# Third layer's feed-forward by rows sorted by position in place of masks, half of its value products on VectorE, and new orders of work

## What is computed

```python
x = L0_attn_representations                     # (2, 1024, 128)
xn = _layernorm(x, axis=-1)
s = _L0_attn_ref(xn, ...)                       # softmax attention, 16 heads, 1024 keys
g = _silu(_L0_ffn_ref(xn, ...))                 # top 2 of 8 experts
x = x + s * g
... L1: linear recurrence, top 2 of 8 experts (hidden 352)
# L2 attention: per token, its 16 heads (of width 8) attend to each other
qkv = jnp.einsum('bnm,fm->bnf', x, Wqkv).reshape(b, n, 16, -1)
scores = jnp.einsum('bnhd,bngd->bnhg', q, k) / SCALE
out = jnp.einsum('bnhg,bngd->bnhd', jax.nn.softmax(scores, axis=-1), v)
return jnp.einsum('bni,mi->bnm', out.reshape(b, n, -1), Wproj) + bproj
# L2 feed-forward: one of 8 matrices, chosen by the token's position alone
idx = jnp.argmax(jnp.einsum('sp,tp->st', pe, jnp.sign(tile_sigs)), axis=-1)
y_all = jnp.einsum('bsd,tod->bsto', x, W) + b
out = take_along_axis(y_all, idx, ...)
... L3: causal attention with decay, top 1 of 8 experts (hidden 512)
```

## Time and profile before

| | |
|---|---|
| median of 3 runs | 991.14 us (988.55 to 994.42) |
| the profiled execution | 985.0 us, its span 983.2 us, granted TensorE clock 0.984 |
| busy: PE, DVE, ACT, POOL | 894.0, 766.7, 537.4, 599.2 us |
| share of the span: PE, DVE, ACT, POOL | 91%, 78%, 55%, 61% |

### The profile page before, as it was taken

How to read it: one execution, slowest core, us unless ns; L and a number is a source line. 1 busy time by engine, 2 the same in 40 slices (tenths; PEclk the granted TensorE clock), 3 DMA queues, 4 the chain that set the end, 5 groups by cost and what they waited for, 6 DMA issues and landing times. The chain is left out here.

```text
span 983.2 us, 20738 instructions
## 1 busy us (share of the span) xinstructions
PE 894.0 (91%) x7627; PEld 471.3 (48%) x7627; DVE 766.7 (78%) x1324; ACT 537.4 (55%) x903; POOL 599.2 (61%) x533
## 2 busy tenths in 40 slices
PE   4899997999999999899998999789999778799996
PEld 2356562233333333233332233679887444478695
DVE  6997789888888888998888852894589999983413
ACT  2154455666766676566666676454365334375463
POOL 3670327668887776878698876106527787572323
PEclk9899998999999999999999999999999999999999
DMA  9362364011111201102111113548761001253562
GB/s 314 117 208 86 105 195 145 16 41 47 32 57 29 65 25 31 49 22 74 40 40 38 40 35 110 169 140 262 217 188 62 23 24 52 68 164 106 161 180 83
DMA packets 90339, 94.86 MB, mean 96 GB/s; under 512 B 23136, under 2 KB 67296, under 8 KB 89984
## 3 DMA queue, kind: packets, MB, share of 16 engines
q1 hardware_dynamic: 85120, 83.04, 27.5%
q0 software_dynamic: 5120, 10.50, 3.7%
HBM read 68.79 MB, written 24.25 MB: 95 GB/s over the span
## 5 line engine op out<-in xcount | busy, mean ns | idle before, releaser
L254 PE MATMUL ps<-ar 64*64 64x512 f32 (+3 forms) x5244 | 518.7, 446 | 28.1 <-DVE small L276 8.9
L254 PEld LDWEIGHTS ps<-ar 64*64 64x64 f32 (+2 forms) x5244 | 254.3, 135 | 275.7 <-ACT ar L300 84.1
L300 ACT ACTIVATE ar<-ps 128x1024 f32<-128x1024 f32 (+1 forms) x302 | 284.0, 944 | 117.5 <-PE ps L254 111.3
L276 DVE TENSOR_REDUCE small<-ps 128x2 f32<-128x1024 f32 (+2 forms) x276 | 306.6, 1139 | 46.6 <-PE ps L254 44.7
L263 POOL TENSOR_TENSOR psum_sb<-psum_sb,ar 128x1024 f32<-128x1024 f32 x91 | 214.8, 2360 | 53.1 <-DVE on_sb L263 41.9
L263 POOL TENSOR_TENSOR ar<-ar 128x512 f32<-128x512 f32 (+1 forms) x80 | 80.0, 1004 | 45.4 <-DVE ar L276 22.3
L322 POOL DMA_INDIRECT gT<-ysort,rt x48 | 48.0, 999 | 92.8 <-issue 91.5
L263 DVE TENSOR_TENSOR ar<-ps,ar 128x256 f32<-128x256 f32 (+4 forms) x48 | 50.5, 1059 | 55.2 <-PE ps L254 51.4
L263 POOL TENSOR_TENSOR psum_sb<-ar 128x1024 f32<-128x1024 f32 x32 | 75.8, 2370 | 23.8 <-ACT ar L300 16.6
L297 ACT COPY ar<-ps 128x256 f32<-128x256 f32 (+2 forms) x84 | 30.8, 378 | 72.7 <-PE ps L254 33.3
L254 PE MATMUL ps<-wA,xnT 128*128 128x512 f32 (+3 forms) x208 | 60.8, 419 | 4.0 <-DVE rt L268 1.8
(11 more groups left out here) (160 smaller groups left out, 1077.2 us busy)
## 6 DMA issues: line engine op xcount, KB each, us to landing
ar<-in_L_up SPq DMA_DIRECT2D x46, 384.0 KB, 4.0
ar<-in_L_b SPq DMA_DIRECT2D x30, 322.0 KB, 3.6
rec_sb<-lscr SPq DMA_DIRECT2D x64, 128.0 KB, 2.9
scr<-ar SPq DMA_DIRECT2D x48, 128.0 KB, 2.6
ar<-xsort SPq DMA_DIRECT2D x36, 128.0 KB, 3.9
ysort<-ar SPq DMA_DIRECT2D x36, 128.0 KB, 1.9
ar<-scr SPq DMA_DIRECT2D x32, 112.0 KB
ar<-scr SPq DMA_DIRECT2D x32, 96.0 KB
```

The source lines that it names most:

```text
L254: return self.e.matmul(o, l, r, start=start, stop=stop) if self.e else Nothing()
L276: return self.e.tensor_reduce(o, a, AX.X, op, negate=True) if negate else self.e.tensor_reduce(o, a, AX.X, op)
L300: return self.e.activation(o, a, fn, **kw) if self.e else Nothing()
```

## The change

The masks of L2's feed-forward go, with `ffn2`, `split` and `combine`. The position's choice is instead routed like an expert (group `BYPOS`), with slots that both halves share; GpSimd scatters the normalised rows (`scat2`), SyncE loads them (`load2`), TensorE turns and multiplies them with one matrix and its bias (`turn2`, `prod2`), ScalarE copies (`xout2`, `yout2`), SyncE stores (`store2`), GpSimd gathers (`gath2`), ScalarE applies Silu (`silu2`). `end2` is now a bias on ScalarE and the blend that the other layers use. VectorE makes the value products of heads 8 to 15 (a new fourth word of `tile`), GpSimd those of 0 to 7. `lnbuf` of L2 has two buffers. All three tables of words are new.

```diff
+BYPOS = NG
+GROUPS += ((2, 0),)
...
+        if layer == 2:
+            return rec_sb[:, 0:512] if c % 2 == 0 else spare[:, 512:1024]
...
-        def ffn2(c):
...
-                    pe.mm(ps[:, b, :], cb_late[:, 128 * e8:128 + 128 * e8], gTT2[:, x_]).then_inc(
...
-                    pe.mm(ps[:, 5, :], w2l[:, 128 * p:128 * p + 128],
-                          psum_sb[:, 512 * (p % 2):512 * (p % 2) + 512], start=p == 0, stop=False).then_inc(
...
+        def turn2(h):
+            for j in range(NTG[BYPOS]):
+                n = NTG[BYPOS] * h + j
+                b = take(ring[0])
+                pe.wait_ge(*vacant(b))
+                pe.wait_ge(*at(f"x2_in{n % 2}", n))
+                for k in range(halves2(j)):
+                    r = slice(128 * k, 128 * k + 128)
+                    ins = pe.tr(ps[:, b, r], xin2[n % 2][:, r], ident)
+                ins.then_inc(*filled(b, ("xT2", n)))
+                yield
...
+        def prod2(h):
...
+                for k in range(halves2(j)):
+                    r, e8 = slice(128 * k, 128 * k + 128), number2[h, j][k]
+                    pe.mm(ps[:, b, r], xT2[n % 2][:, r], w2l[:, bass.ds(e8, 128)], stop=False)
+                    ins = pe.mm(ps[:, b, r], cb_late[0:96, bass.ds(e8, 128)], bias2b[0:96, :], start=False)
...
+            pe.wait_ge(*at(f"tile{k}_dve", i, "av"))
             pe.wait_ge(*at(f"tile{k}_pool", i, "av"))
...
-            dve.stt(acc_sb[:, 1024:1536], ps[:, bank["proj2", c], :], M("bp"), gT[:, cols(c)], ALU.add,
-                    ALU.mult).then_inc(*emptied(("proj2", c), ("gated", 2, c)))
-            yield
-            combine(2, c)
+            blend(2, c)
...
-                dve.tt(xb, x_, ps[:, bank["spread", c, e8], :], ALU.mult).then_inc(
-                    *emptied(("spread", c, e8), ("xb", c, e8)))
...
+            dve.wait_ge(*at(t, i, "shares"))
+            if i >= 2:
+                dve.wait_ge(*at("tileT", i - 2))
...
+            for h in range(8, 16, 4):
+                ins = dve.tt(pr2[k].rearrange("p (g h d) -> p h g d", g=16, d=8)[:, h:h + 4, :, :],
+                             s3_.unsqueeze(3)[:, h:h + 4, :, :].to_broadcast([128, 4, 16, 8]),
+                             qkv[k][:, 256:384].rearrange("p (g d) -> p g d", d=8).unsqueeze(1).to_broadcast([128, 4, 16, 8]),
+                             ALU.mult)
+            ins.then_inc(*up((t, i, "av")))
...
+        def end2(c):
+            act.wait_ge(*at("proj2", c))
...
+            act.af(acc_sb[:, 1024:1536], ps[:, bank["proj2", c], :], ACT.Identity, bias=M("bp")).then_inc(
+                *emptied(("proj2", c), ("s2", c)))
...
+        def scat2(h):
+            pool.wait_ge(*at("route_dve", BYPOS, "slots"))
+            pool.wait_ge(*at(f"clear2{h}_in", 0))
+            for c in (2 * h, 2 * h + 1):
+                pool.wait_ge(*at("xnT", 2, c))
...
+        def gath2(h):
...
+            for i in range(8):
+                pool.wait_ge(*at("x", 2, 2 * h + i // 4))
...
+                if i in (40, 48):
+                    clear(i == 48, xsort2, NHALF[BYPOS] * HALF, "clear2")
```

More of the change, by code:

```diff
@@ L538, in _program @@
     ysort = [nc.dram_tensor(f"ysort{h}", [NHALF[0] * HALF, 128], F32).ap() for h in range(2)]
+    xsort2, ysort2 = ([nc.dram_tensor(f"{n}sort2{h}", [NHALF[BYPOS] * HALF, 128], F32).ap() for h in range(2)] for n in "xy")
     rt = sb("rt", [128, 768])
@@ L561, in _program @@
     st2 = [area(QKV + 1280 + 64 * k, 64) for k in range(2)]
-    gTT2 = osb_[:, 0:512].bitcast(BF16)
+    xin2 = [psum_sb[:, 256 * k:256 * k + 256] for k in range(2)]
+    xT2 = [psum_sb[:, 512 + 256 * k:768 + 256 * k] for k in range(2)]
+    yrow2 = [spare[:, 256 * k:256 * k + 256] for k in range(2)]
     w2l = on_sb[:, :]
@@ L575, in _program @@
     s3b = [acc_sb[:, 512 * i:512 * i + 512] for i in range(2)]
-    bp2 = [wA[:, MISC_N + 128 + 64 * i:MISC_N + 192 + 64 * i].bitcast(BF16) for i in range(3)]
+    bias2b, bmid = (wA[:, MISC_N + 128 + 64 * i:MISC_N + 192 + 64 * i].bitcast(BF16) for i in range(2))
     btmp = wA[:, MISC_N:MISC_N + 128]
@@ L713, in ln @@
             ins.then_inc(*filled(b, ("xnT", layer, c)))
-        def split_transposes(n, c0, key):
-            g24 = v3(gsp, 24)[:, c0 // 128:c0 // 128 + n, :]
-            b = take(ring[0])
-            pb = ps[:, b, :].bitcast(BF16)
-            pe.wait_ge(*vacant(b))
-            pe.wait_ge(*at("split_dve", *key))
-            for j in range(n):
-                ins = pe.tr(pb[0:24, 128 * j:128 * j + 128], g24[:, j, :], identb)
-            ins.then_inc(*filled(b, ("splitT", *key)))
         def qk(c, ty):
@@ L873, in tail0 @@
                 yield
-        def combine(layer, c, a):
-            b = take(ring[0])
-            pe.wait_ge(*vacant(b))
-            pe.wait_ge(*at("gated", layer, c))
-            for j in range(4):
-                ins = pe.tr(ps[:, b, 128 * j:128 * j + 128], a[:, 128 * j:128 * j + 128], ident)
-            ins.then_inc(*filled(b, ("delta", layer, c)))
         def end0(c):
@@ new lines, in position, with numbers2 @@
+            b = take(ring[0])
+            pe.wait_ge(*vacant(b))
+            pe.wait_ge(*at("route_dve", BYPOS, "chosen"))
+            pe.mm(ps[:, b, 0:64], below, ohs[:, 0:64])
+            pe.mm(ps[:, b, 128:192], onesb, ohs[:, 0:64]).then_inc(*filled(b, ("ranks", BYPOS)))
+        number2 = {}
+        def numbers2(h, j):
+            number2[h, j] = pe.numbers(nc, experts[BYPOS][0:1, 2 * j:2 * j + 2], (NE - 1) * STRIDE[2])
+        def turn2(h):
+            for j in range(NTG[BYPOS]):
+                n = NTG[BYPOS] * h + j
+                b = take(ring[0])
+                pe.wait_ge(*vacant(b))
+                pe.wait_ge(*at(f"x2_in{n % 2}", n))
[4 more added lines that the diff above has]
+                yield
@@ new lines, in prod2 @@
+        def prod2(h):
+            for j in range(NTG[BYPOS]):
+                n = NTG[BYPOS] * h + j
+                if j == 0:
+                    pe.wait_ge(*at("experts", BYPOS))
+                    numbers2(h, 0)
+                b = take(ring[0])
+                pe.wait_ge(*vacant(b))
+                pe.wait_ge(*at("xT2_sb", n))
+                pe.wait_ge(*at("late_in", 0))
+                pe.wait_ge(*at("bias2", 0))
+                for k in range(halves2(j)):
+                    r, e8 = slice(128 * k, 128 * k + 128), number2[h, j][k]
+                    pe.mm(ps[:, b, r], xT2[n % 2][:, r], w2l[:, bass.ds(e8, 128)], stop=False)
+                    ins = pe.mm(ps[:, b, r], cb_late[0:96, bass.ds(e8, 128)], bias2b[0:96, :], start=False)
+                ins.then_inc(*filled(b, ("y2", n)))
+                if j + 1 < NTG[BYPOS]:
+                    numbers2(h, j + 1)
+                yield
@@ L1161, in tensor_program @@
                   "end0": end0, "end1": end1, "end2": end2, "tables": tables, "rec": rec, "position": position,
-                  "ffn2": ffn2, "tile": tile, "att3": att3, "state3": state3, "end3": end3, "route": route}
+                  "turn2": turn2, "prod2": prod2, "tile": tile, "att3": att3, "state3": state3, "end3": end3, "route": route}
         follow(ORDER_A["tensor"], stages)
@@ L1827, in ln @@
                 act.wait_ge(*at("ln_pool", layer, c, "offset"))
-                if layer == 2 and c > 0:
-                    act.wait_ge(*at("xnT", layer, c - 1))
+                if layer == 2 and c >= 2:
+                    act.wait_ge(*at(f"sorted2{c % 2}", c - 2))
                 if layer == 3 and c >= 2:
@@ L2121, in scalar_program @@
         stages = {"xout": x_out, "silu": silu, "hout": h_out, "ln": ln, "qk": qk, "max0": max0, "tail0": tail0,
[L2122 removed]
+                  "xout2": xout2, "yout2": yout2, "silu2": silu2, "end2": end2, "tile": tile, "att3": att3, "state3": state3, "l3start": l3start, "route": route, "gather": gather,
                   "silu0": silu0, "rows": rows}
@@ L2329, in gather @@
                     yield
-        def clear2():
-            pool.wait_ge(*at("scaled", 30))
-            pool.memset(osb_[:, 0:512], 0.0).then_inc(*up(("clear_g", 0)))
-            yield
+        def scat2(h):
[3 more added lines that the diff above has]
+                pool.wait_ge(*at("xnT", 2, c))
+                for i in range(4):
+                    t = 4 * (c % 2) + i
+                    pool.scatter(xsort2[h], slots[BYPOS][:, t:t + 1], lnbuf(2, c)[:, 128 * i:128 * i + 128]).then_inc(
+                        *landed((f"sorted2{c % 2}", c) if i == 3 else (f"sorted2{c % 2}",)))
+                yield
+        def gath2(h):
+            last_n = NTG[BYPOS] * h + NTG[BYPOS] - 1
+            for n in (last_n - 1, last_n):
+                pool.wait_ge(*at(f"y2_out{n % 2}", n))
+            for i in range(8):
+                pool.wait_ge(*at("x", 2, 2 * h + i // 4))
+                pool.gather(gT[:, 128 * (8 * h + i):128 * (8 * h + i) + 128], ysort2[h], slots[BYPOS][:, i:i + 1]).then_inc(
+                    *landed((f"rows2_in{i}", h, i)))
+                yield
         feed0()
```

(22 more changed lines are left out.)

160 lines of the change are left out of this document (63 added, 97 removed), and 277 rows, old and new, of tables (ORDER_A, ORDER_C, SIDE_B).

## The result

The changed kernel takes 1005.23 us (median of 8 runs, 999.42 to 1007.62), the kernel before 988.54 us in the runs beside it (8 runs, 984.84 to 994.42): a ratio of 1.0154, 95% interval 1.0119 to 1.0189. The prediction was 987 us with a range up to 1001. The profiled execution has a span of 1003.1 us against 983.2, so there are 19.9 us to account for.

What follows compares the result with a forecast made beforehand. VectorE was taken to bound the third layer until its last shares, then a GpSimd and TensorE chain. Terms -1.5 - 2 - 0.4 = -3.9 on 985.0 give 981.1, scaled to 987 us; range 973 to 1001.

Steps and rivals of the forecast that it cites:

- What bounds the kernel now: Third layer: VectorE is the bound until its last shares (881.83), then a chain through GpSimd and TensorE to 898.86; 176.65 us.
- What is taken away, what is added: Third layer: VectorE swaps 32 masks (18.9 us) for 32 value products (20.5); TensorE gets 12 us against 46.3 removed.
- The price of sharing: VectorE's value products stretched beside GpSimd's, both reading SBUF: 0.7 us for 10 tiles, 7 us; bounds 0 and 21.6.
- The end of the third layer: Old waits of 6 us shrink to 3.3, tail about 8.3; layer 169.3 us without contention, 176.3 with: -0.4.
- Rival 1: Full contention on VectorE's value products: 17.5 us instead of 7, third layer +10.1, whole 998 us; chance 0.20.
- Rival 3: Round trip of the second half's rows sets the pace, TensorE waits and last Silu is 8 us late: 992 us; chance 0.10.
- Rival 4: TensorE's clock: more gaps put sums at the lower clock, delaying tiles by some 10 us: 996 us; chance 0.05.
- The other stages: First stage -1.5 us (-4 to +2), 605 to 722 us -2 (-6 to +2), last layer 0 (-2 to +3).

Runs made afterwards that it cites:

- the two repeated layers: Third-layer lengths of two kernel pairs: 196.02 us with the last stores apart against 197.88 in the changed kernel; 177.12 with early orders alone against 176.65 in the kernel before.

## Why the prediction was wrong

- **What bounds the kernel now**: right for the kernel before, where VectorE worked 152.80 of 159.62 us. It does not carry over whole: in the new order the layer follows what is taken from VectorE's stretched products, but not what is taken by giving products back to GpSimd (a quarter on VectorE: 16 us less busy than in the changed kernel, 7 of the layer; none: 30 less, and 9 longer).
- **What is taken away, what is added**: right for VectorE. 16.5 + 18.4 us aside, it did 154.8 us of work up to its last value product, and I had counted 157.7. On TensorE I expected some 25 us less busy time; it was 4.7 less (146.53 for 151.26), at a granted clock of 0.87 in place of 0.96. No run shows that the layer hung on it.
- **The price of sharing** is the term that failed first: "I take half of it, 0.7 for 10 tiles: 7 us". It was 1.2 a pair for 11 pairs, 12.9 us, and 3.6 more on the recurrence's products, 16.5 in sum. The count of meetings was right; the one row that showed the meeting showed nearly the price, and the discount for GpSimd's lateness had no row behind it. The Trainium skill ("SBUF — State Buffer", Who interferes with whom) says that a VectorE instruction with two SBUF inputs contends with GpSimd's reads of SBUF, and the stretched pairs agree; it says that one with at most one SBUF input, outside the two-port modes, does not, and the products with one input in PSUM agree at 0.68 us. A hold of the shared ports for the whole instruction, which I priced at 2.2 us a pair, is said there of VectorE's two-port modes; for these products it was too much for all but the worst.
- **The end of the third layer** failed next, and by more: "Of the 6 us of old waits about 3.3 stay". 18.4 us of idle time stand ahead of the last value product. The tail behind it was right (8.15 us, forecast 8.3). VectorE was busy for 88% of the layer (174.62 of 197.88 us), where I expected over 93%. I took the value products for work like the masks, and gave them no waits of their own. As a step in each tile's chain they came with more: 14.3 us of idle time with the split alone and all masks in place, 14.9 with all four on VectorE. That the masks had filled such gaps is not shown. Leaving out the rows took 5.6 us of idle time off the layer (190.94 - 173.24 against 197.88 - 174.62). Why the waits grew so much stays open beyond that. These two terms are +9.5 and +15.1; the work, overcounted by 2.9, brings the sum to the 21.6 by which 197.9 misses 176.3.
- **Rival 1** had the right mechanism and 998 us: it lacked the waits. That its 17.5 us come so near to 16.5 is partly luck, since 3.6 of these lie on products that it did not count. **Rival 3** did not happen on TensorE (no wait for rows at 856.81), though leaving out the rows shortens the layer by 6.9 us. **Rival 4**: the clock fell further, to 0.73 in 815 to 840, but filling TensorE, which raised it from 0.87 to 0.93 over the layer, didn't help.
- **The other stages**: -4.55 against -3.5, near, but within what the start of the layer varies by from run to run, so it can be luck; the last stretch 0 (-2 to +3) against +3.2, just outside its bounds.

How the 21.2 us divide: 8.2 go with the stretching of 24 products, 3.7 more with the rows, and 9.4 stay, of which the other eight products can be 5.4. Each figure is the difference of two single executions, good to some 2 us by the two repeated layers. What was not tried is the sorted rows in the old order of tiles, so that their own worth there stays open, and so does the part of the new order.

## What to carry to other kernels

Before work moves to an engine, look in the trace for a place where the same two kinds of operation have met, and take the price that stands there, near in full: here 1.2 us a pair of the 1.35 seen. Work of the same length is not the same work in an order: a mask waited for a spread alone, a value product stands in the chain of its tile, and in three kernels that had it on VectorE that engine idled 14.3 to 18.4 us where 6.8 had been. Where a product must be split over VectorE and GpSimd, one input in PSUM on VectorE's side kept it at 0.68 us, where those with both in SBUF took 1.28 on the mean.

## What the runs showed of the hardware

VectorE's products with both inputs in SBUF were stretched by GpSimd's products (1.5 to 3.4 us a pair for 1.28), not by its gathers (1.28 at 793.50); there the gather took 1.34 us for 0.94. GpSimd paid 0.14 us a product, VectorE 0.40 on the mean of its 32 value products. Sharing 64 products saved VectorE little: 40.2 us on its line for 37 products beside GpSimd's 32, 44.7 for 69 without them.
